# Four small attention layers: the order of work in front of their first block

## The reference

```python
x = x + attn(layernorm(x))
q = rms_or_layer_norm(x @ Wq + bq); k = ...; v = ...        # 4 to 32 heads of 8 or 16
p = softmax(where(mask, q @ k.T * scale, -inf))
out = (p @ v) @ Wo + bo
```

## Time and profile before

| | |
|---|---|
| runs of the kernel | 3345.0 us median of 3 (3343.33 to 3359.64) |
| the profiled execution | 3354.53 us, its span 3352.7 us |
| PE busy | 2892.6 us, 86% of the span |
| DVE, ACT, POOL busy | 2244.6, 1844.5 and 1733.3 us |
| l0x | from 179.3 us to about 480 |
| l1a | from 597.7 us to about 745 |
| l2a | from 1330.1 us to 1556.7 |
| l2x | from 1556.7 us to about 1842 |

### The profile page before, as it was taken

How to read it: one execution, slowest core, us unless ns; L and a number is a source line. 1 busy time by engine, 2 the same in 40 slices (tenths; PEclk the granted TensorE clock), 3 DMA queues, 4 the chain that set the end, 5 groups by cost and what they waited for, 6 DMA issues and landing times. The chain is left out here.

```text
span 3352.7 us, 71643 instructions
## 1 busy us (share of the span) xinstructions
PE 2892.6 (86%) x25174; PEld 2211.4 (66%) x25209; DVE 2244.6 (67%) x5446; ACT 1844.5 (55%) x3541; POOL 1733.3 (52%) x1835
## 2 busy tenths in 40 slices
PE   7959989689999864796677899799999799998898
PEld 5737765457778553564455555688888688887565
DVE  5567754756777712884786677566666577777787
ACT  3336753346666321463665565466666577775575
POOL 1122211214555464563773367688888588886232
PEclk9979999799999776898899899899999999999899
DMA  4010010000000344000000632000000000000001
GB/s 157 1 22 13 13 58 13 7 5 8 7 6 3 110 114 89 5 6 22 15 15 11 244 87 65 3 0 0 0 0 1 7 7 5 5 5 12 17 25 38
DMA packets 93886, 102.31 MB, mean 31 GB/s; under 512 B 41500, under 2 KB 80860, under 8 KB 90719
## 3 DMA queue, kind: packets, MB, share of 16 engines
q1 hardware_dynamic: 89064, 93.98, 9.2%
q0 software_dynamic: 4608, 5.57, 1.0%
HBM read 80.84 MB, written 11.61 MB: 28 GB/s over the span
## 5 line engine op out<-in xcount | busy, mean ns | idle before, releaser
L1905 PE MATMUL bank<-l3a_ln_xnT,far 128*128 128x128 f16 x3072 | 185.8, 221 | 1.8 <-POOL l3a_ln_xnT L1721 1.8
L1905 PEld LDWEIGHTS bank<-l3a_ln_xnT,far 128*128 128x128 f16 x3072 | 180.8, 99 | 3.4 <-POOL l3a_ln_xnT L1721 2.2
L877 PE MATMUL bank<-l2f_xnT,l2f_wi 128*128 128x512 f16 x672 | 157.1, 382 | 7.0 <-POOLq L741 6.4
L388 DVE SCALAR_TENSOR_TENSOR x_res<-bank,l3f_combine,x_res 128x256 f32<-128x256 f32 x320 | 132.8, 477 | 26.3 <-PE bank L541 24.1
L3180 PE MATMUL bank<-l0x_v,l0x_pT 128*128 128x128 f32 x1024 | 134.3, 279 | 3.1 <-ACT l0x_pT L3598 1.5
L3180 PEld LDWEIGHTS bank<-l0x_v,l0x_pT 128*128 128x128 f32 x1024 | 127.3, 192 | 13.8 <-issue 4.7
L2789 POOL TENSOR_TENSOR l1x_prob<-l1x_prob,l1x_srec 128x512 f32<-128x512 f32 x64 | 67.8, 1060 | 122.0 <-DVE l1x_srec L2560 122.0
L541 PE MATMUL bank<-l3f_wd,l3f_h 128*128 128x256 f16 x960 | 119.4, 275 | 11.2 <-DVE l3f_h L380 11.2
L541 PEld LDWEIGHTS bank<-l3f_wd,l3f_h 128*128 128x128 f16 x960 | 94.5, 99 | 40.4 <-DVE l3f_h L380 12.0
L531 PE MATMUL bank<-l3f_xnT,l3f_wi 128*128 128x512 f16 x480 | 120.4, 389 | 0.4 <-issue 0.4
L877 PEld LDWEIGHTS bank<-l2f_xnT,l2f_wi 128*128 128x128 f16 x672 | 65.3, 98 | 78.3 <-POOLq L741 9.9
(11 more groups left out here) (727 smaller groups left out, 9392.1 us busy)
## 6 DMA issues: line engine op xcount, KB each, us to landing
far<-in_l1f_in SPq DMA_DIRECT2D x32, 256.0 KB, 3.8
l2f_front<-l2f_shares SPq DMA_DIRECT2D x5, 1024.0 KB, 4.9
sums<-near SPq DMA_DIRECT2D x2, 2176.0 KB, 19.3
far<-in_l1f_down SPq DMA_DIRECT2D x32, 128.0 KB, 4.4
l1f_xn<-sums SPq DMA_DIRECT2D x32, 128.0 KB, 2.3
l2f_wi<-in_l2f_in SPq DMA_DIRECT2D x14, 256.0 KB, 5.9
far<-l0x_kT SPq DMA_DIRECT2D x64, 48.0 KB
far<-l2x_kT SPq DMA_DIRECT2D x32, 96.0 KB
```

The source lines that it names most:

```text
L388: last = nc.vector.scalar_tensor_tensor(core.x[:, b, :], y, combine[:, b, bass.ds(n, 1)], core.x[:, b, :], ALU.mult, ALU.add)
L877: last = nc.tensor.matmul(bank[:, :], wi16[n % 2][p][:, a, k, :], xnT[q][:, k, 512 * g:512 * g + 512], start=(k + p + q == 0), stop=(k == ...
L1905: last = nc.tensor.matmul(bank[:, P * j:P * j + P], w(k, 512 * c + P * j, P, p), norm.xnT[u][q][:, k, :], start=(k + p + q == 0), stop=(k ...
```

## The change

In every small attention layer, the head is taken apart and its pieces go between the first pipeline steps.

- DVE: the head is empty. `weights_part` (centring of weights, `centred`, low halves, `w_ready`) runs at the end of the first step, behind `moments(0)`. `tables_part` (wait for `tables_in`, masks, centring of biases, angles, `tables_ready`) runs at the end of the third step. DVE clears nothing any more.
- ACT: the high halves of the weights come first. `clear`, at the end of the second step, writes zeros over `diagonal` and `q2X` with one instruction; `angles`, the sines, is at the end of the third; the wait for `zeroed` is ahead of the fourth.
- POOL: only `c16` is cleared first. Its other clearing, with the wait for `tables_in`, is in the second step.
- PE: the wait for `tables_ready` is at the first scores; `project_ctx(0)` waits for `w_ready`.

The diff, without the lines that are only moved or indented:

```diff
+        to_clear = core.far[:, 0:sum(taken)]
...
                 def project_ctx(b):
+                    if b == 0:
+                        pe.wait_ge(w_ready, 1)
                     pe.wait_ge(c_split, b + 1)
...
                     after(pe, found, f - 1)
+                    if f == 0:
+                        pe.wait_ge(tables_ready, 1)
...
-                pe.wait_ge(tables_ready, 1)
...
-                for t in diagonal + (q2X if spread else []):
-                    nc.vector.memset(t, 0.0)
-                dve.drain().then_inc(cleared, 1)
-                dve.wait_ge(tables_in, 16 * sum(len(t[2]) for t in tables.values()))
...
+                def weights_part():
+                    dve.wait_ge(loaded[0], loaded[1])
+                    if split:
...
+                        centre(by_head(weights["q"]), 32)
+                        centre(keys, 32)
+                    dve.drain().then_inc(centred, 1)
...
+                    dve.drain().then_inc(w_ready, 1)
...
+                def tables_part():
+                    dve.wait_ge(tables_in, 16 * sum(len(t[2]) for t in tables.values()))
...
+                    dve.drain().then_inc(tables_ready, 1)
...
+                    if s == STEPS[0]:
+                        weights_part()
+                    if s == STEPS[2]:
+                        tables_part()
 
             @block.scalar
             def _(act):
-                if kind == "axial":
+                def clear():
+                    if kind != "summed":
+                        nc.scalar.activation(to_clear, core.ones[:, 0:1].to_broadcast(list(to_clear.shape)), ACT.Copy,
+                                             scale=0.0).then_inc(cleared, 1)
+
+                def angles():
...
-                act.wait_ge(zeroed, 1)
                 for s in STEPS:
+                    if s == STEPS[3]:
+                        act.wait_ge(zeroed, 1)
...
+                    if s == STEPS[1]:
+                        clear()
+                    if s == STEPS[2] and kind == "axial":
+                        angles()
 
             @block.gpsimd
             def _(pool):
...
+                def clear_ctx():
...
+                def clear():
...
+                    pool.drain()
                     pool.wait_ge(tables_in, 16 * sum(len(t[2]) for t in tables.values()))
...
-                if not split:
-                    pool.wait_ge(tables_in, 16 * sum(len(t[2]) for t in tables.values()))
+                clear_ctx()
                 for s in STEPS:
...
                     if wg is not None:
                         rsqrt(wg)
+                    if s == STEPS[1]:
+                        clear()
```

More of the change, by code:

```diff
@@ L3250, in _ @@
-                if kind == "axial":
[L3252 to L3261, removed]
-                        nc.vector.tensor_copy(whole[:, :, :], turns[:, :, :])
-                        dve.drain()
-                        nc.vector.tensor_copy(turns[:, :, :], whole[:, :, :])
-                        dve.drain()
-                        nc.vector.scalar_tensor_tensor(angle[:, :, :], turns[:, :, :], -2 * PI, angle[:, :, :],
-                                                       ALU.mult, ALU.add)
-                        for op, bound, step in ((ALU.is_gt, PI, -2 * PI), (ALU.is_lt, -PI, 2 * PI)):
@@ L3303, in _ @@
-                dve.drain().then_inc(tables_ready, 1)
+                            nc.vector.tensor_copy(whole[:, :, :], turns[:, :, :])
+                            dve.drain()
+                            nc.vector.tensor_copy(turns[:, :, :], whole[:, :, :])
+                            dve.drain()
+                            nc.vector.scalar_tensor_tensor(angle[:, :, :], turns[:, :, :], -2 * PI, angle[:, :, :],
+                                                           ALU.mult, ALU.add)
+                            for op, bound, step in ((ALU.is_gt, PI, -2 * PI), (ALU.is_lt, -PI, 2 * PI)):
+                                dve.drain()
+                                nc.vector.tensor_scalar(turns[:, :, :], angle[:, :, :], bound, step, op, ALU.mult)
+                                dve.drain()
+                                nc.vector.tensor_tensor(angle[:, :, :], angle[:, :, :], turns[:, :, :], ALU.add)
@@ L3707, in _ @@
-                pool.drain().then_inc(zeroed, 1)
+                def clear_ctx():
+                    if split:
+                        for u in range(2):
+                            nc.gpsimd.memset(c16[u][:, :, :, :], 0.0)
+                        pool.drain()
+                def clear():
+                    for u in range(NZ):
+                        nc.gpsimd.memset(zq[u][:, :, :], 0.0)
+                        nc.gpsimd.memset(zk[u][:, :, :], 0.0)
+                    for u in range(NV):
+                        nc.gpsimd.memset(v_all[u][:, :], 1.0)
+                    pool.drain()
+                    pool.wait_ge(tables_in, 16 * sum(len(t[2]) for t in tables.values()))
+                    for a in range(parts):
+                        for u in range(NZ):
+                            if split:
+                                nc.gpsimd.tensor_scalar(zk[u][:, :, KS + a], consts["part"][:, a:a + 1].to_broadcast(
+                                    [P, HK]), SHIFT, None, ALU.mult)
+                            else:
+                                nc.gpsimd.memset(zk[u][:, :, KS + a], SHIFT)
+                        if split:
+                            for u in range(NV):
+                                nc.gpsimd.tensor_copy(v[u][:, :, (HD + 1) * (a + 1) - 1],
+                                                      consts["part"][:, a:a + 1].to_broadcast([P, HV]))
+                    pool.drain().then_inc(zeroed, 1)
```

93 lines of the change are left out of this document (37 added, 56 removed).

## The result

| | before | after |
|---|---|---|
| median of 5 runs each | 3348.77 us (3343.33 to 3359.64) | 3324.45 us (3322.10 to 3332.12) |
| ratio | | 0.9922, 95% interval 0.9901 to 0.9942 |
| profiled execution, span | 3354.53, 3352.7 | 3327.55, 3325.8 |

The forecast was 3325.4 (3314 to 3337), so the time is 0.95 us off. The gain by medians is 24.3 us, where the sum had 19.6.

The account below looks back on a forecast made before the run. The prediction took each changed layer's gain to be how much earlier its first blocks come, if they keep that lead: 4.7 + 7.4 + 3.0 + 4.5 = 19.6 us off 3345.0, giving 3325.4 us, range 3314 to 3337.

Parts of the forecast that it names:

- the sum: All four changed layers: gains of 4.7, 7.4, 3.0 and 4.5, together 19.6 us.
- Each layer runs at a pace that the change doesn't touch: Four changed layers once the pipeline has filled: pace unchanged, so only earlier first blocks count; no size of its own.
- l1a: Layer l1a: third normalise at 607.7 instead of 612.39, decided by POOL's clearing, bias and rsqrt; gain 4.7 us.
- l2a: Layer l2a: normalise(0) no longer waits for the tables, 1333.8 instead of 1341.24; gain 7.4 us.
- l2x: Layer l2x: context split 7.1 us earlier, but POOL's clearing and filling then delay normalise(1); gain 3.0 us.
- In l2x DVE has 4 us to spare: Layer l2x: DVE idles some 4 us ahead of normalise(1), so POOL's clearings holding DVE up cost nothing.
- l0x: Layer l0x: first queries 8.9 us earlier, less 4.4 for POOL's clearings holding DVE up beside the angles; gain 4.5 us.
- slips in after each clearing: l0x angles: one DVE operation gets in after each of nine POOL clearings, 6.6 us for 2.2 of work, 4.4 lost.
- No hold (1): l0x: POOL's clearing doesn't hold DVE up; 4.4 us more there, 24 in all, 3321 us; chance 0.35.
- The lead lost through the clock (2): Downstream, TensorE's clock rises no earlier, so half or more of the lead goes; gain some 8, 3337 us; chance 0.14.
- Slower (3): Clock stays at half level well into the full pipeline; kernel 20 us slower, 3365 us; chance 0.03.
- blocked for longer (4): A new order blocks another engine longer than reckoned (l2x gains 0, l1a 2); gain 13, 3332 us; chance 0.03.

Follow-up runs that it names:

- act_fills: Changed kernel, but in l0x and l2x ACT instead of POOL clears zq and zk and fills v; 3316.94 us, ratio 0.9883.
- one_drain: Changed kernel with one POOL drain ahead of the row of clearings and none between them; 3332.30 us in one run.
- combined: act_fills for l0x and l2x; in l1a and l2a POOL clears zq, zk and v ahead of the first rstd; 3317.09 us, ratio 0.9897.
- drains: Changed kernel with a POOL drain behind each clearing; 3337.35 us in one run.
- warm: combined plus unread matrix products in PE's idle time at the heads and filling steps of l0x, l1a, l2a and l2x; 3317.32 us, ratio 0.9894.
- tables_first: Changed kernel, but in l1a, l2a and l2x DVE's tables_part, with its wait, is back in the first step; 3339.21 us in one run.
- warm_three: warm without its unread products in l2x; 3313.73 us, ratio 0.9877.

## Why the prediction was right, and where not

**What bounds it.** "The gain of a layer is by how much its first blocks come earlier, if they keep that lead" is borne out by the table above. "Each layer runs at a pace that the change doesn't touch" fell in three places: l1a's later blocks, l1f, where 5.7 us were gained while the clock stood higher, in a layer that nobody changed, and l3f, where 3.1 were lost while it stood lower. No term of the sum had this.

**l1a**, 4.7 forecast: the third `normalise` was to come 10.0 behind the start and came at 10.4, waiting for POOL 1.82 us where "about a microsecond" was said. The mis-sized term is POOL's clearing: 3.6 us (597.80 to 601.43) where 2.9 was taken. That is 4.3 earlier than before, and the length 6.2 shorter in the mean. At the same milestones two other kernels were at 152.7 and 152.9, so the clock gave some of it.

**l2a**, 7.4 forecast, 7.0 measured: `normalise(0)` at 3.6 (3.5 forecast). The missing 0.4 is a step that I hadn't got: `normalise(0)` itself met POOL's clearings and took 1.29, so the read came at 9.35 instead of 8.7.

**l2x**, 3.0 forecast, 3.5 measured. The context was there 10.8 behind the start, as reckoned, and POOL behind the split decided. The term was mis-sized: clearing and filling took 8.4 (1545.69 to 1554.11) and not 9.1, and began 0.3 earlier, so `normalise(1)` led by 4.1. "In l2x DVE has 4 us to spare" was true ahead of `normalise(1)`, where 2.10 us were left in spite of the hold, but not ahead of the first read: the hold was 5.85 us and made that late by some 1.4 (18.7 against 17.3 in `act_fills`). It cost nothing, as POOL was later still.

**l0x**, 4.5 forecast, 5.3 measured. DVE's list was earlier than reckoned (angles from 5.8 instead of 6.9). The hold was 5.0 where I took 4.4, between 0 and 5.3. The mechanism was half right. DVE and POOL do stand in each other's way, but in after no operation "slips in after each clearing": the whole row is one hold. `one_drain` shows the picture I had drawn, with 3.4 lost (10.6 instead of 7.2). That 4.4 came so near to 5.0 is luck. The long write of ACT took 5.32, within 5.1 to 6.2, and the copy and the load behind it cost nothing. PE's first product came 9.3 behind the start, a little ahead of the 9.7 to 10.7 forecast.

By the Trainium skill, "SBUF — State Buffer", section "Who interferes with whom", the second to issue blocks until the first is through. The trace agrees that a `tensor_scalar` blocks, but not that the end of the first frees it: in l0x one operation was blocked through all seven clearings (4.58 us), in `one_drain` through one (0.89).

**Rivals.** No hold (1): the forecast of a first read at 15 is what `act_fills` gave (15.6), and after gave 19.1. It falls. The lead lost through the clock (2) did not come true for the kernel, as all four layers kept their lead, but its mechanism is real: `combined` gained 1.8 us at the front of l1a and lost it at 0.51, and `one_drain` lost 1.6 of l0x at 0.83. Slower (3) and blocked for longer (4) didn't occur.

**The size.** The time was right to a microsecond partly by two errors that cancel: the gain was 4.7 us over the sum by medians, while before stood 3.8 higher in this comparison (3348.77) than in the three runs of the forecast (3345.0). Those three were low: over the 32 times of the kernel before in all rounds, on more than one chip, the median is 3354.6, and the two traced executions of it, 3354.53 and 3356.12, lie there too. From that the sum would have given 3335, and the gain would be 30. So the four terms of the sum, 19.6 against the 22.0 of the layers, are the sounder part, and that the time is right to a microsecond is luck.

Open is why l1f's clock stands at 0.53 to 0.56 in its second 20 us in before, `drains` and `warm`, and at 0.86 to 0.95 in the others. It was the same in both traces of before, of after and of `warm`, and isn't a matter of l1a's length (`tables_first`, with the longest l1a, has 0.92). `warm` and `warm_three` differ only in code that runs behind l1f, so it isn't set by the code ahead alone. Open is also why l3f's clock is lower after, and what begins and ends a hold.

## What to carry to other kernels

Look for what the first block of a layer waits for, and take out of DVE's and POOL's heads all that it doesn't need; a microsecond there was a microsecond of the layer in three of four. Don't queue long clearings of POOL back to back while DVE scales and converts: write them with ScalarE if it is idle, or put them at the head. When a kernel's heads shift, compare the lengths and the granted clock of the layers that were not changed before giving a gain or a loss to the edit.

## What the runs showed of the hardware that I had not expected

- A hold of DVE by POOL can run through a whole row of POOL's writes, up to 5.85 us for a 0.17 us operation. A drain behind every clearing cut it to one clearing at a time, 0.75 to 0.99 us in l0x. One drain ahead of the row did the same in l0x (0.89 to 0.95) and nothing in l2a (1.48, without it 1.29).
- ACT writes 6144 columns in 5.32 us, 3072 in 2.76 and 512 in 0.6, and beside the write of 6144 columns DVE's rows keep their 0.23 and POOL's first clearing its 0.95.
- An unchanged layer, l1f, was 5.7 us shorter in both traces of after, with 0.86 instead of 0.54 of the clock over 20 us, though the 356 us of another unchanged layer, l1x, lie between it and the reordered code. Another, l3f, was 3.1 us longer, with 0.74 instead of 0.89.
- Unread matrix products in the idle head brought the clock to 0.94 from 0.51 between 20 and 48 us of l1a, and the layer from 151.1 to 146.4 us (0.82, 148.5 and 147.0 us in two other traces).
